# The first dense expert's two matrix products, split into two of 64 tokens each, for the lower and the upper output partitions in alternation

## The chip, the cores and the metric

The kernel is written in Bass, instruction by instruction for each engine, and runs on one core of a Trainium2 chip. The metric is the time of one execution on the device in microseconds (us), taken as the median of several runs. Rows of the profile come from one further execution that was recorded by the hardware profiler.

## The reference

A gated block on x of shape (4, 256, 256), that is 1024 tokens of 256 channels, in float32. First an additive adjacency step, then a mixture of experts with 32 experts of which each token uses 6, and a shared expert:

```python
x = x + tanh(g_xattn[0]) * L0_xattn_ref(ctx_512, layernorm(x), W, b)      # 0.6*sigmoid(si + sj + b) + 0.4*adj
x = x + tanh(g_ffn[0]) * L0_ffn_ref(layernorm(x), ...)
...
scores = sigmoid(xf @ w_router)                  # T = 1024 tokens, E = 32 experts
...                                              # best 4 of 8 groups, then best 6 experts in them
g = einsum('th,ehm->etm', xf, gate_w)            # H = 256, M = 176
u = einsum('th,ehm->etm', xf, up_w)
eo = einsum('etm,emh->eth', silu(g) * u, down_w)
routed = einsum('te,eth->th', combine, eo)
shared = silu(xf @ sh_gate_w) * (xf @ sh_up_w) @ sh_down_w
return routed + shared
```

## The kernel before

Tokens are handled 128 at a time (P = 128, J = 8 blocks). After the first residual step, the router and the shared expert, each token's row is scattered by GpSimd (`place`, L439) into a table in DRAM, `rows_dram`, once for each of its chosen experts, so that the rows of one expert lie together. Then the experts' work is done in **tiles** of 128 rows of one expert: ScalarE's queue fetches a tile (`load`, L282), TensorE transposes it (`transpose_x`, L759), multiplies it with the expert's gate and up weights (`gate_up`, L765), transposes the product (`turn_h`, L773) and multiplies it with the down weights (`down`, L779). ScalarE scales the result (L565), and GpSimd adds it into one of three sums in DRAM (`add`, L451). There are some 50 such tiles, ten to a round.

Two experts are left out of the tiles and treated **densely**, for all 1024 tokens, with a weight of zero where a token didn't choose them. The kernel finds the two that are used most. The first of them, which the change touches, is run **before** the tiles, straight from the transposed tokens `xnT`, by `gate_up_busy`, `turn_h_busy` and `down_busy`; the second after the tiles (L864, L873, L884).

For block j of 128 tokens of the first dense expert:

- `gate_up_busy(j)` makes 128 tokens by 352 columns (176 of gate, 176 of up) in the PSUM bank `pG[j % 2]`. The tokens (`xnT`) are the operand that TensorE loads as weights, 128 channels by 128 tokens; the expert's weights `busy_gu` are streamed past them. The 256 channels make two steps (k = 0, 1) that add up in PSUM.
- ScalarE takes the silu of the gate half (L569), VectorE multiplies (`gate_busy`, L1207).
- `turn_h_busy(j)` transposes the product in two steps of 88 columns (L796), and VectorE copies it into `hT` (L1211).
- `down_busy(j)` makes 128 tokens by 256 columns in `pY[j % 2]`, in two steps of 88 (L807). VectorE adds it to the tokens (`add_busy`, L1217).

TensorE's order in this stage is `gate_up_busy(0)`, and then for each j: `gate_up_busy(j + 1)`, `turn_h_busy(j)`, `down_busy(j - 1)`; the transposes of the first two tiles stand ahead of the last `down_busy`. Each engine works its own instructions in the order written and waits for others by semaphores.

In the trace's names several buffers share memory: `xg` in a row of L788 is `busy_gu`, `wd` in L807 is `busy_d`, `sup` is `hT`, `sdown` is `xT`, `sgate` is `sg` and `h`, `wgu` in rows ahead of the tiles is a buffer of the first step or of the shared expert. A row's operands carry their partitions and columns: 128*64 are weights of 64 columns. Each product of float32 appears in the trace as **two passes**, each with a load of weights (a row of PEld) and a MATMUL (a row of PE). So the two steps of one `gate_up_busy` are four passes, and so are those of one `down_busy`.

Some small products elsewhere serve as prices in what follows: products of the identity at the start (L629), transposes of ctx with 64 columns of weights (L635), the adjacency's scores (L645 with one streamed column, L648 with 256), and the table of tiles (L750 with 2 columns of weights, L752, L753). The program gives L635 the array's tile of 128 rows by 64 columns and L750 that of 128 by 32, both at column 0, and L629, L752 and L753 the whole array.

Two transfers hang on the end of this stage. SyncE's last group of expert weights waits for `s_by` to reach J, that is for the last `down_busy`, since their place is shared with `busy_d`. And ScalarE's queue issues the load of the fifth tile (`load(act, JH, JH)`) only behind the copies of the first two transposed tiles:

```python
            copy_xT(0, 0)
            copy_xT(1, 1)
            load(act, JH, JH)
            silu(0, 0)
```

Of the kernel before, what the change touches and what calls it, by code (L numbers as in the profile page):

```python
# [14 lines left out]
P = 128  # L15
# [16 lines left out]
def gated_xattn_moe(nc, x, ctx, g_xattn, g_ffn, w_adj, b_adj, w_router, corr_bias, gate_w, up_w, down_w,  # L32
                    sh_gate_w, sh_up_w, sh_down_w, out):
    B, N, H = x.shape
    D = ctx.shape[2]
    E, _, M = gate_w.shape
# [3 lines left out]
    K = H // P  # L40
    I = 2
    MI = M // I
# [28 lines left out]
    INTO_LAST = [0, 2, 1, 0, 2, 1, 0, 2, 1, 0]  # L71
    LEFT = sorted(range(SUMS), key=lambda i: max(s for s in range(ROUND) if INTO_LAST[s] == i))

    SECOND = [3, 5, 6, 7]
    PLACED = [range(0, GROUP), range(GROUP, JH), range(JH, J)]

    with ExitStack() as stack:
        def sb(name, shape, dt=F32):
            return stack.enter_context(nc.sbuf_tensor(name, shape, dt))

        def bank(name):
            return stack.enter_context(nc.psum_tensor(name, [P, 512], F32))
# [22 lines left out]
        xnT = sb("xnT", [P, K, T])  # L105
# [82 lines left out]
        hT = sup[:, :, :].rearrange("p k m -> p (k m)")[:, 0:4 * P].rearrange("p (a k t) -> p a k t", a=2, k=2)  # L188
# [5 lines left out]
        busy_gu = xg_own[:, :, :].rearrange("p i c -> p (i c)")[:, 0:2 * K * M].rearrange("p (g k m) -> p g k m", g=2, k=K)  # L194
        busy_d = wd[:, E - BATCH, :, :]
# [14 lines left out]
        pG = [bank(f"pG{i}") for i in range(2)]  # L210
        pH = [bank(f"pH{i}") for i in range(2)]
        pY = [bank(f"pY{i}") for i in range(2)]
# [171 lines left out]
        def _(pool):  # L384
# [37 lines left out]
            def second_rstd(b):  # L422
                g = slice(b * GROUP, (b + 1) * GROUP)
                pool.wait_ge(s_var, SECOND[b])
                pool.tensor_tensor(out=rstd2[:, g], in0=rstd2[:, g], in1=power[:, g], op=ALU.pow).then_inc(s_rstd, 1)
# [199 lines left out]
        def _(pe):  # L625
# [8 lines left out]
            for j in range(J):  # L634
                ins = nc.tensor.transpose(pX[j // 4][0:D, (j % 4) * P:(j % 4 + 1) * P], ctx_sb[:, j, :], ident[:, :])  # L635
# [6 lines left out]
            for c in range(2):  # L642
                pe.wait_ge(s_ctxTc, c + 1)
                for j in range(c * JH, (c + 1) * JH):
                    ins = nc.tensor.matmul(si_banks[c][:, j:j + 1], ctxT[:, j * P:(j + 1) * P], wij[:, 0:1], start=True, stop=True)  # L645
# [139 lines left out]

            def gate_up_busy(j):
                for k in range(K):
                    ins = nc.tensor.matmul(pG[j % 2][:, 0:2 * M].rearrange("t (g m) -> t g m", g=2),  # L788
                                           xnT[:, k, j * P:(j + 1) * P], busy_gu[:, :, k, :],
                                           start=(k == 0), stop=(k == K - 1))  # L790
                ins.then_inc(s_bgu, 1)

            def turn_h_busy(j):
# [6 lines left out]
            def down_busy(j):  # L800
                pe.wait_ge(s_bhTc, j + 1)
                if j < 2:
                    pe.wait_ge(s_shyc, J - 1 + j)
                else:
                    pe.wait_ge(s_byc, j - 1)
                for i in range(I):
                    ins = nc.tensor.matmul(pY[j % 2][:, 0:H], hT[0:MI, j % 2, i, :], busy_d[:, i, :],  # L807
                                           start=(i == 0), stop=(i == I - 1))
                ins.then_inc(s_by, 1)

            pe.wait_ge(s_busyw, 64)
            gate_up_busy(0)
            for j in range(J):
                if j + 1 < J:
                    gate_up_busy(j + 1)
                turn_h_busy(j)
                if j:
                    down_busy(j - 1)
            pe.wait_ge(s_tiles, 1)
            transpose_x(0, 1, 0)  # L820
            transpose_x(1, 1, 1)
            down_busy(J - 1)
            e_first = look_up(0)
            pe.wait_ge(s_ready, e_first + 1)
# [77 lines left out]
        def _(dve):  # L902
# [55 lines left out]
            def norm_group(b):  # L958
                dve.wait_ge(s_rstd, SECOND[b])
                for j in range(b * GROUP, (b + 1) * GROUP):  # L960
                    V.tensor_scalar(xn[:, j, :], xs[:, j, :], mv[:, j, 0:1], rstd2[:, j:j + 1],
                                    ALU.subtract, ALU.mult).then_inc(s_xn, 1)
# [345 lines left out]
```

## Time and profile before

| what | us |
|---|---|
| median of 3 runs | 249.18 (248.64 to 250.74) |
| the profiled execution's own time | 250.6 |
| its span, first to last instruction | 248.7 |
| TensorE busy in the span | 225.7 (91%) |
| first dense expert on TensorE, from its first pass to the first pass of the tiles | 67.48 to 86.24 |

The span is what the rows below divide. A busy time of TensorE counts from the start of a pass to its modelled end, and passes overlap, so the starts tell more than the durations.

### The profile page before, as it was taken

To read this page: it belongs to the slowest core of one execution; us is meant where nothing else is said; L and a number is where in the kernel's file an instruction comes from. 1 tells how busy PE (TensorE), PEld (TensorE's weight loads), DVE (VectorE), ACT (ScalarE), POOL (GpSimd) and SP (SyncE) were. 2 spreads that over 40 slices of the span, in tenths; PEclk is the share of its full clock that TensorE was granted. 3 is DMA by queue.
4 is the path that set the end of the run, shared out by engine and by line. 5 is a ranking of instruction groups with operands and counts; after the bars stand their busy time and mean duration, and the time that the engine had idled before them with its cause. 6 is when DMAs were issued, how large, how long until landed. Compare 5 with 4: busy or idle time off the path is not lost.

```text
span 248.7 us, 4830 instructions
## 1 busy us (share of the span) xinstructions
PE 225.7 (91%) x1051; PEld 175.0 (70%) x1052; DVE 130.5 (52%) x523; ACT 78.2 (31%) x220; POOL 137.1 (55%) x133
## 2 busy tenths in 40 slices
PE   7994998996899977988899999999999899999980
PEld 6893786884677754765677777777777678777760
DVE  2898588989744541333343434343434334442765
ACT  3635122110021121313435353444444344433220
POOL 6253747777777752344565657565656547565000
PEclk9778699999799996899999999999999999999996
DMA  6999999999999999799765658677666634447846
GB/s 203 279 284 304 407 372 346 319 359 329 337 374 344 367 227 327 164 269 227 141 110 116 112 103 154 111 130 105 114 108 121 104 36 59 55 55 116 259 138 225
DMA packets 39290, 51.67 MB, mean 208 GB/s; under 512 B 4942, under 2 KB 33710, under 8 KB 39270
## 3 DMA queue, kind: packets, MB, share of 16 engines
q1 hardware_dynamic: 24368, 29.81, 39.1%
q0 software_dynamic: 10416, 17.20, 34.1%
q10 hardware_dynamic: 4486, 4.44, 6.8%
q8 instruction: 7, 0.11, 0.2%
q14 instruction: 13, 0.11, 0.1%
HBM read 30.83 MB, written 20.61 MB: 207 GB/s over the span
## 4 chain that ended last, share of the span: by engine, by line
PE 67%; DVE 16%; DMA 5%; issue 4%; ACTq 3%; ACT 3%; POOL 1%; DVEq 1%
PE pG L765 21%; PE pY L779 15%; PE pG L704 5%; PE pX L759 4%; PE pH L773 4%; PE pG L864 4%; PE pG L788 4%; DMA xg<-rows_dram 3%; PE pY L715 3%; PE pY L807 2%; PE pY L884 2%; DVE xs L1267 2%; DMA wij<-in_L_xattn_W_dram 1%; ACTq L267 1%; ACTq L282 1%
## 5 line engine op out<-in xcount | busy, mean ns | idle before, releaser
L451 POOL DMA_INDIRECT sum_dram<-choice,idx x50 | 77.4, 1548 | 59.2 <-ACT choice L565 42.9
L765 PE MATMUL pG<-wgu,sdown 128*128 x200 | 69.8, 472 | 3.8 <-ACT sdown L553 2.8
L439 POOL DMA_INDIRECT rows_dram<-rows,row_i x48 | 47.0, 980 | 19.0 <-issue 14.1
L779 PE MATMUL pY<-wd,sup 88*128 x200 | 52.3, 384 | 0.0
L1193 DVE COPY sup<-pH 88x256 f32<-88x256 f32 x50 | 21.0, 420 | 55.1 <-PE pH L773 55.1
L765 PEld LDWEIGHTS pG<-wgu,sdown 128*128 128x128 f32 x200 | 35.1, 195 | 16.6 <-issue 6.2
L565 ACT ACTIVATE choice<-pY,wt 128x256 f32<-128x256 f32 x50 | 23.7, 473 | 55.3 <-PE pY L779 30.9
L779 PEld LDWEIGHTS pY<-wd,sup 88*128 88x128 f32 x200 | 34.6, 193 | 3.1
L773 PEld LDWEIGHTS pH<-ident,sgate 128*88 128x88 f32 x100 | 16.0, 161 | 12.5 <-issue 0.6
L558 ACT ACTIVATE sgate<-pG 128x176 f32<-128x176 f32 x50 | 15.9, 317 | 24.4 <-PE pG L765 23.6
L553 ACT ACTIVATE sdown<-pX 128x256 f32<-128x256 f32 x50 | 18.7, 376 | 7.9 <-PE pX L759 5.2
L773 PE MATMUL pH<-ident,sgate 128*88 128x128 f32 x100 | 19.4, 276 | 0.0
L1189 DVE TENSOR_TENSOR sgate<-sgate,pG 128x176 f32<-128x176 f32 x50 | 16.2, 325 | 5.9 <-ACT sgate L558 5.9
L704 PE MATMUL pG<-xnT,sgate 128*128 128x256 f32 (+1 forms) x48 | 14.6, 432 | 0.0
L715 PE MATMUL pY<-sdown,wgu 128*128 128x256 f32 (+1 forms) x48 | 12.8, 423 | 0.6 <-DVE wgu L1069 0.6
L704 PE MATMUL pG<-xnT,sup 128*128 128x256 f32 (+1 forms) x48 | 13.3, 403 | 0.0
L525 ACT ACTIVATE wgu<-pG 128x256 f32<-128x256 f32 (+1 forms) x12 | 4.6, 383 | 27.5 <-PE pG L704 27.5
L759 PEld LDWEIGHTS pX<-ident,rows 128*128 128x128 f32 x60 | 11.4, 196 | 2.0 <-issue 0.6
L715 PEld LDWEIGHTS pY<-sdown,wgu 128*128 128x128 f32 (+1 forms) x48 | 10.2, 214 | 2.5 <-DVE wgu L1069 0.8
L759 PE MATMUL pX<-ident,rows 128*128 128x128 f32 x60 | 11.6, 278 | 0.2 <-issue 0.2
L704 PEld LDWEIGHTS pG<-xnT,sup 128*128 128x128 f32 (+1 forms) x48 | 9.5, 198 | 2.1
L864 PE MATMUL pG<-wgu,xnT 128*128 x32 | 10.8, 460 | 0.0
(188 smaller groups left out, 275.9 us busy)
## 6 DMA issues: line engine op xcount, KB each, us to landing
wgu<-in_L_ffn_gate_w_dram SPq DMA_DIRECT2D x8, 704.0 KB, 10.8
wgu<-in_L_ffn_up_w_dram SPq DMA_DIRECT2D x8, 704.0 KB, 11.4
wd<-in_L_ffn_down_w_dram SPq DMA_DIRECT2D x8, 640.0 KB
sum_dram<-zeros POOLq DMA_DIRECT2D x3, 1152.0 KB, 13.1
rows<-rows_dram ACTq DMA_DIRECT2D x18, 144.5 KB, 3.6
rows_dram<-zeros SPq DMA_DIRECT2D x8, 289.0 KB, 3.9
rows<-sum_dram SPq DMA_DIRECT2D x8, 256.0 KB, 3.8
xg<-rows_dram ACTq DMA_DIRECT2D x12, 144.5 KB, 2.8
```

What stands on the lines that cost most here:

```text
L439: pool.indirect_dma_start(rows_dram[:, :], bass.IndirectOffsetOnAxis(ap=row_i[:, j, k:k + 1], axis=0), rows[:, j, :], None).then_inc(done, 16)
L451: pool.indirect_dma_start(sums_dram[into[s]][:, :], bass.IndirectOffsetOnAxis(ap=idx[:, s:s + 1], axis=0), y[s % YRING], None, compute_op= ...
L553: nc.scalar.activation(xT[:, par, :, :].rearrange("p k t -> p (k t)"), pX[par][:, 0:K * P], ACT.Copy).then_inc(s_xTc, 1)
L565: nc.scalar.activation(y[s % YRING], pY[s % 2][:, 0:H], ACT.Copy, scale=wt[:, s:s + 1]).then_inc(s_yc, 1)
L704: ins = nc.tensor.matmul(pG[u % 2][0:m, i * GROUP * P:(i + 1) * GROUP * P], w[:, k, c], xnT[:, k, b * GROUP * P:(b + 1) * GROUP * P], star ...
L715: ins = nc.tensor.matmul(pY[j % 2][:, 0:H], sh[0:m, b % 2, i, (j % GROUP) * P:(j % GROUP + 1) * P], sdown[0:m, i, :], start=(i == 0), stop ...
L759: ins = nc.tensor.transpose(pX[par][:, k * P:(k + 1) * P], xg[s][:, 0:H].rearrange("t (p k) -> t k p", k=K)[:, k, :], ident[:, :])
L765: ins = nc.tensor.matmul(pG[par][:, 0:2 * M].rearrange("t (g m) -> t g m", g=2), xT[:, par, k, :], wgu[:, bass.ds(e, 1), :, k, :].rearrang ...
L773: ins = nc.tensor.transpose(pH[par][0:MI, i * P:(i + 1) * P], h[:, par, :].rearrange("t (p i) -> t i p", i=I)[:, i, :], ident[:, :])
L779: ins = nc.tensor.matmul(pY[par][:, 0:H], hT[0:MI, par, i, :], wd[:, bass.ds(e, 1), i, :], start=(i == 0), stop=(i == I - 1))
L864: ins = nc.tensor.matmul(pG[j % 2][:, 0:2 * M].rearrange("t (g m) -> t g m", g=2), xnT[:, k, j * P:(j + 1) * P], wgu[:, bass.ds(e_common, ...
L1193: V.tensor_copy(hT[0:MI, par, :, :].rearrange("p i t -> p (i t)"), pH[par][0:MI, 0:I * P]).then_inc(s_hTc, 1)
```

## The change

Each product of `gate_up_busy` and of `down_busy` becomes two, one for tokens 0 to 63 of the block, which fills partitions 0 to 63 of the PSUM bank, and one for tokens 64 to 127, which fills partitions 64 to 127. For each step k (or i) the lower half is issued and then the upper half. Each half loads 64 columns of weights in place of 128, and streams the same 352 (or 256) columns past them. The program gives these halves the tile of 128 rows by 64 columns of TensorE's array, the lower at column 0 and the upper at column 64; all other products of the dense expert have the whole array of 128 by 128. Which instruction signals the other engines stays the same: the last of each group.

```diff
+    PARTED = [slice(0, P // 2), slice(P // 2, P)]
...
             def gate_up_busy(j):
                 for k in range(K):
-                    ins = nc.tensor.matmul(pG[j % 2][:, 0:2 * M].rearrange("t (g m) -> t g m", g=2),
-                                           xnT[:, k, j * P:(j + 1) * P], busy_gu[:, :, k, :],
-                                           start=(k == 0), stop=(k == K - 1))
+                    for part in PARTED:
+                        ins = nc.tensor.matmul(pG[j % 2][part, 0:2 * M].rearrange("t (g m) -> t g m", g=2),
+                                               xnT[:, k, j * P + part.start:j * P + part.stop], busy_gu[:, :, k, :],
+                                               start=(k == 0), stop=(k == K - 1))
                 ins.then_inc(s_bgu, 1)
...
                 for i in range(I):
-                    ins = nc.tensor.matmul(pY[j % 2][:, 0:H], hT[0:MI, j % 2, i, :], busy_d[:, i, :],
-                                           start=(i == 0), stop=(i == I - 1))
+                    for part in PARTED:
+                        ins = nc.tensor.matmul(pY[j % 2][part, 0:H], hT[0:MI, j % 2, i, part], busy_d[:, i, :],
+                                               start=(i == 0), stop=(i == I - 1))
                 ins.then_inc(s_by, 1)
```

On TensorE, from the shared expert's last product (`shared_down(3)`) into the third block of the dense expert, the order before is this (a row gives the line, output<-operands, output partitions x columns, and how many in a row):

```order
L715 MATMUL pY<-sdown,wgu 128x256 x6
L788 MATMUL pG<-xg,xnT 128x352 x4
L796 MATMUL pH<-ident,sgate 88x128 x2
L788 MATMUL pG<-xg,xnT 128x352 x2
L796 MATMUL pH<-ident,sgate 88x128 x2
L807 MATMUL pY<-wd,sup 128x256 x2
L788 MATMUL pG<-xg,xnT 128x352 x2
```

and after the change, at the same place (line numbers below the diff's first hunk are one higher, below the second two, and below the third three):

```order
L716 MATMUL pY<-sdown,wgu 128x256 x6
L790 MATMUL pG<-xg,xnT 64x352 x8
L798 MATMUL pH<-ident,sgate 88x128 x2
L790 MATMUL pG<-xg,xnT 64x352 x4
L798 MATMUL pH<-ident,sgate 88x128 x2
L810 MATMUL pY<-wd,sup 64x256 x4
L790 MATMUL pG<-xg,xnT 64x352 x4
```

Nothing changes its place. Every product of L788 and L807 stands twice, with 64 output partitions in place of 128. The other engines' instructions and their order are the same.

## Rows read from the trace of the kernel before

**Rows 1.** The page's first part: busy time, share of the span, instructions.

```profile
PE 225.7 (91%) x1051; PEld 175.0 (70%) x1052; DVE 130.5 (52%) x523; ACT 78.2 (31%) x220; POOL 137.1 (55%) x133
```

**Rows 2.** The chain that ended last: start us, us, what released the next.

```profile
86.50 8.10 DMA xg<-rows_dram
94.64 0.70 PE pX L759 x2
...
95.63 2.71 PE pG L765 x4
98.34 0.43 PE pH L773 x2
98.76 1.71 PE pY L779 x4
...
125.24 1.19 PE pG L765 x4
126.64 0.87 PE pY L779 x4
...
239.50 0.49 DVE xs L1256
```

**Rows 3.** TensorE's timeline from the dense expert on: start us, us, line, operation, idle before.

```profile
70.07 1.35 PE L788 MATMUL pG<-xg,xnT 128*128 128x352 f32 x4
71.25 0.38 PE L796 MATMUL pH<-ident,sgate 128*88 128x128 f32 x2
71.47 1.03 PE L807 MATMUL pY<-wd,sup 88*128 88x256 f32 x4
72.34 1.35 PE L788 MATMUL pG<-xg,xnT 128*128 128x352 f32 x4
...
91.04 1.03 PE L779 MATMUL pY<-wd,sup 88*128 x4
94.64 0.70 PE L759 MATMUL pX<-ident,xg 128*128 128x128 f32 x2 [2.57 <-DMA xg<-rows_dram]
```

**Rows 4.** TensorE's timeline at the start, same columns.

```profile
1.50 2.93 PE L629 MATMUL pH<-ident 128*128 128x128 f32 x12 [1.50 <-POOL ident L400]
4.22 1.81 PE L635 MATMUL pX<-ident,wgu 128*64 128x128 f32 x8
```

**Rows 5.** Line L635's passes: durations min/median/max ns, first and last start us.

```profile
L635 PE MATMUL pX<-ident,wgu x8: 313/421/421, 4.2 to 5.7; 128*64 128x128 f32 x8
```

**Rows 6.** Timeline again: products of one streamed column (PE), a group of weight loads (PEld).

```profile
6.27 1.05 PE L645 MATMUL pX<-wij,xnT 64*128 64x1 f32 x8
7.18 1.11 PE L648 MATMUL pG<-xnT,wj_wide 64*128 64x256 f32 x4
...
69.96 0.89 PEld L788 LDWEIGHTS pG<-xg,xnT 128*128 128x128 f32 x4
```

**Rows 7.** TensorE's timeline at the tile table, just before the dense expert.

```profile
61.75 0.27 PE L750 MATMUL pH<-ident,tile_of 128*2 128x128 f32 x1 [2.33 <-DVE tile_of L1171]
61.86 0.38 PE L752 MATMUL pH<-ident,limit 128*128 128x128 f32 x2
62.08 0.39 PE L753 MATMUL pH<-ident,low 128*128 128x128 f32 x2
```

**Rows 8.** ScalarE's tile loads (L282): four issued from 70 to 78, four from 86 to 93.

```profile
DMA to landing us min/median/max: 6.4/6.8/7.1
...
DMA to landing us min/median/max: 6.6/7.0/7.4
```

**Rows 9.** Stretches: busy time by engine, granted TensorE clock, DMA share, GB/s.

```profile
64.00:65.00 1.00, 1.00 (x4) 0.82 (x3) 0.93 (x4) 0.00 (x0) 0.69 (x2) 0.50 1.04 367
...
95.00:100.00 5.00, 4.72 (x12) 2.95 (x11) 1.00 (x4) 0.70 (x2) 1.61 (x1) 0.50 0.78 278
```

**Rows 10.** TensorE's timeline at the end of the tile loop's steady part.

```profile
197.64 0.50 PE L759 MATMUL pX<-ident,rows 128*128 128x128 f32 x2 [0.25 <-issue]
198.74 1.45 PE L765 MATMUL pG<-wgu,sdown 128*128 x4 [0.61 <-issue]
```

## The prediction

> **What bounds the kernel now.** I read the page's first part, then the chain that ended last, then TensorE's timeline of the stage that the change touches, and last the rows elsewhere that price a pass, a load of weights and a change of tile. TensorE is busy for 225.7 of 248.7 us [rows 1], and the chain shows that it is no mere average: inside the tile loop it goes from `gate_up` to `down` and back in turns of 2.5 us, and only the last sums, from 239.50 on, are VectorE's [rows 2]. In the dense stage TensorE never waits: four passes of `gate_up_busy` take 71.25 - 70.07 = 1.18 us, two transposes 0.22, four passes of `down_busy` 72.34 - 71.47 = 0.87, and the next turn starts without a gap [rows 3]. So whatever this stage gains or loses on TensorE moves its end at 86.24 by as much.
>
> Behind it stands the only slack. The fifth tile's load is issued at 86.50, behind the copies of the first two transposed tiles, and lands 8.10 us later [rows 2]. TensorE is out of work at 91.04 + 1.03 = 92.07, 5.57 after that issue, and waits 2.57 us [rows 3]. Then the granted clock is at its half level, 1.2 GHz (0.50) [rows 9]: the next `gate_up` takes 2.71 against 1.19, the transposes 0.43 against 0.22, the `down` 1.71 against 0.87 [rows 2, 3]. That is 1.52 + 0.21 + 0.84 = 2.6 us lost to the clock.
>
> **What a half costs by itself.** A pass streams as many columns as before; the question is whether 64 output tokens stream faster than 128. They don't: eight passes of L635, which load 64 columns, start 4.2 to 5.7, 0.21 us apart [rows 5], and twelve passes of L629 just before, of 128 columns and as many streamed, fill 1.50 to 4.22, 0.23 apart with the slow first one in it [rows 4]. So a half costs a whole pass, 0.295 in `gate_up_busy` and 0.217 in `down_busy`, and there are now 64 of each in place of 32. One after the other, that is 8 x 1.18 + 8 x 0.87 = 16.4 us more. All depends on whether the upper half streams while the lower one does.
>
> No row of this trace has a product at column 64 of the array, so I bound it. If the halves overlap, TensorE still takes its instructions in order: lower step 0, first pass and second pass, then upper, first and second. Both passes of a half use the same columns of the array, so the second waits for the first. What can overlap is the second pass of one half with the first of the next. A block of products with nothing before it then has starts at 0, p, p, 2p, 2p and so on (p is the length of a pass): as fast as before, but its last pass streams alone. The chip leaves this mode ten times (the products stand in ten runs between transposes; seven end in a `gate_up_busy`, three in a `down_busy`), which costs 7 x 0.295 + 3 x 0.217 = 2.7 us. That is the lower bound with overlap.
>
> To it comes the load of weights. A load starts when the pass before it has started and not earlier: the first load for a `gate_up_busy` begins at 69.96, 0.11 before its product at 70.07, when the second transpose pass begins [rows 3, 6]. Where a product streams only one column, loads set the pace: (7.18 - 6.27) / 8 = 0.114 for 128 columns [rows 6]. I take half of it, 0.057, for 64. In the changed stage the upper half's first pass waits that long after the lower half's second has begun, and so on at each of the 64 changes from half to half: 64 x 0.057 = 3.65, and the lone last passes count 0.057 less each: 7 x 0.238 + 3 x 0.160 = 2.15. The sum is **5.8 us**. With a load that costs as much as 128 columns it would be 8.9; with loads pulled ahead, 2.7.
>
> The Trainium skill, "TensorE: Matmul & The Clock Gate", Part 3, says that products in different column tiles run at once, start some 4 ns apart and measured 2.38 times faster for three of them; by its 4 ns the sum would be an estimated 2.9 us. No run here shows it yet.
>
> **What hides it.** The other engines have a turn of 2.27 us (70.07 to 72.34) for one block, and follow later, not sooner: no new wait. The load of the fifth tile and SyncE's last expert weights (which wait for the last `down_busy`) are issued later with the stage, and meet each other again. But the load stands ahead of the last `down_busy`, which grows by 0.39 (5 x 0.217 + 3 x 0.057 - 0.87), so TensorE now wants the tile 5.96 after the issue. Eight loads beside such weights landed in 6.4 to 7.4 us where the trace tells it [rows 8], this one in 8.1. I take 7.4, the slowest of the three others in the same burst. The wait is then 1.4 in place of 2.57: 1.1 back. With 8.1 it is 0.4 back, with 6.4 it is 2.1.
>
> Does the clock still fall? It was at 0.50 behind waits of 2.57 [rows 3, 9] and 2.33 [rows 7, 9], and passes keep their full pace behind waits of 0.25 and 0.61 [rows 10]. A wait of 1.4 lies between; I take it that it falls, as the long ones are the nearer in kind (a stage that has run dry), and give the other answer to a rival. The sum: 5.8 - 1.1 = **4.7 us later**.
>
> **The rivals.**
>
> (a) The halves overlap as above, but the clock holds: 4.7 - 2.6 = 2.1 later, 251.3. For it: most loads landed in 7 us or less, which makes the wait one of 1.0. Against it: the load in question was the slowest.
>
> (b) The halves don't overlap at all: the change doesn't do what its alternation is there for. 16.4 later on TensorE. GpSimd's scatters, which share the transfers, are over by then, so the wait may go altogether, and the slow clock with it: 16.4 - 2.57 - 2.6 = 11.2, up to 15.5 if only the longer last `down_busy` (0.87) is won back; 260.4 to 264.7, some 262. For it: nothing in this trace shows two products at once. Against it: passes already overlap with loads and with each other's ends [rows 3, 6].
>
> (c) A change of tile empties the array. The trace speaks against it: L635 has a tile of 64 columns and starts at 4.22, while the last whole-array pass before it ends at 4.43 [rows 4], and L752 starts at 61.86, 0.16 before the end of L750's tile of 32 columns, just as L753 starts 0.16 before L752's end [rows 7]. If it did, a pass's tail beyond its streaming (1.35 - 4 x 0.295 = 0.17 [rows 3]) would stand bare at 20 changes, 3.4 us: 8.1 later, 257.3. This rule is in the Trainium skill, "TensorEngine Tiling (Array Packing)", Key Properties: changing the tiling mode drains TensorE. By that rule the rows would show a gap that they don't, for a mode that stays at column 0.
>
> (d) Faster than before. The place is the fifth tile's load, the price the wait and the slow clock behind it, 2.57 + 2.6 = 5.2 us. If loads are pulled ahead (2.7 lost) and the tile lands within 6 us, the kernel ends 2.5 earlier, 246.7. It decides as soon as the stage loses less than 5.2 and the wait is gone; the loads' shortest time of 6.4 speaks against the second.
>
> **How the numbers follow.** The profiled execution took 250.6, its span and 1.9 around it; the median is 249.18, 1.4 below. The shifts are differences of the span, and I put them on the median: 249.2 + 4.7 = **253.9**. Chances: the forecast 0.34, (a) 0.26, (b) 0.25, (c) 0.08, (d) 0.07. A measurement of this kernel tells about 1% (2.5 us) from no change. Of (a) I count 0.06 as slower, since its loads may cost more (up to 8.9 in place of 5.8), the rest as the same; of (d) 0.04 as faster. So slower 0.34 + 0.25 + 0.08 + 0.06 = 0.73, the same 0.23, faster 0.04. The range reaches from 249.8, in the midst of what (a) may give with short loads, to 265, the end of (b); it leaves out (d) and the lower part of (a), and little above.
>
> **What would show it.** In the profile after, the passes at column 64 start 0.05 to 0.06 behind the lower half's second pass if the forecast is right, a whole pass behind if (b). The first pass of the transposes starts a whole pass, and no more, behind the last product (more: (c)). The dense stage, 18.76 us now, takes 24.5; 35 under (b), 21.5 under (d). The wait for the fifth tile is near 1.4, and the clock behind it 0.50; under (a) it stays at 1.00. The tile loop's turns of 2.5 us and the tail stay as they are. I am wrong if TensorE holds a half back for another reason (the order of the two passes of a product, the PSUM bank that both halves write), or if the granted clock falls within the stage.

## The result and the profile after

| what | before | after |
|---|---|---|
| median, us | 249.06 (20 runs, 246.2 to 252.61) | 252.39 (20 runs, 249.09 to 254.92) |
| the profiled execution's own time and its span, us | 250.6 and 248.7 | 250.42 and 248.6 |
| first dense expert on TensorE, first pass to first pass of the tiles | 67.48 to 86.24: 18.75 | 66.88 to 88.55: 21.67 |

The kernel became slower by 1.3%: the ratio is 1.0126, with a 95% interval of 1.0086 to 1.0167, that is 3.1 us (2.1 to 4.2). The medians are over all 20 runs, while the ratio leaves out those in a slower state of the chip (six of the kernel after), so it is a little below 252.39 / 249.06. The two profiled executions happen to be equally long, so the cause isn't read from their spans. It is read stage by stage, from the first pass of one stage to the first pass of the next, and checked against the medians.

The page's first part of the kernel after answers to [rows 1]. There are 64 more passes, 1115 in place of 1051, and TensorE is busy as long as before. Halves that streamed one behind the other would have added 16.4 us, so already here the second half of each product seems to cost no streaming of its own. (The two sums can't be compared to less than a few us, since the granted clock over the span was 0.944 before and 0.981 after.)

```profile
PE 225.8 (91%) x1115; PEld 170.0 (68%) x1116; DVE 130.3 (52%) x523; ACT 78.3 (31%) x220; POOL 137.3 (55%) x133
```

TensorE in the dense expert answers to [rows 3]. The first row is of the line's passes (durations min/median/max ns), the second of the timeline in a narrow stretch around the start of a `gate_up_busy`, the others of the timeline over a whole turn (start us, us, line, operation, count, idle before).

```profile
L790 PE MATMUL pG<-xg,xnT x64: 457/459/511, 66.9 to 83.7; 128*64 128x352 f32 x64
...
72.42 0.47 PE L790 MATMUL pG<-xg,xnT 128*64 128x352 f32 x2
...
72.42 1.35 PE L790 MATMUL pG<-xg,xnT 128*64 128x352 f32 x8
73.70 0.46 PE L798 MATMUL pH<-ident,sgate 128*88 128x128 f32 x2
74.09 1.08 PE L810 MATMUL pY<-wd,sup 88*64 88x256 f32 x8
75.01 1.35 PE L790 MATMUL pG<-xg,xnT 128*64 128x352 f32 x8
```

Eight passes of `gate_up_busy` take 1.35 us from start to end, exactly what four took before. The first two rows show why: a pass lasts 0.459, and two of them lie in 0.47. The lower and the upper half start 0.006 us apart (0.005 to 0.008 over all pairs of the stage) and stream together. But a turn lasts 75.01 - 72.42 = 2.59 in place of 2.27, and all of that sits at the seams, the places where split products meet transposes or whole products: 1.28 from the first product to the transposes (1.18 before), 0.39 over the two transposes (0.22), 0.92 over the down products (0.87). The loads of weights of the same turn show the first two of these:

```profile
73.02 0.14 PEld L790 LDWEIGHTS pG<-xg,xnT 128*64 128x64 f32 x2 [0.15 <-issue]
73.70 0.24 PEld L798 LDWEIGHTS pH<-ident,sgate 128*88 128x88 f32 x2 [0.55 <-issue]
74.09 0.20 PEld L810 LDWEIGHTS pY<-wd,sup 88*64 88x64 f32 x4
```

The pair of passes to which the loads of 73.02 belong starts at 73.31 and streams for 0.295, to 73.61. The transposes' load starts only at 73.70, at the same time as its product, 0.094 behind that end; within one shape such a load begins 0.11 ahead, when the pass before has just started [rows 3, 6]. Then the transposes' second pass follows 0.187 behind the first where 0.11 was usual, since its load too comes only now. Into the down products it is the same again. The number of loaded columns alone isn't the cause: before, products with 128 loaded columns and transposes with 88 follow each other without a gap [rows 3].

Behind the stage, TensorE at the tiles and the chain that ended last (start us, us, what released the next) answer to the ends of [rows 2, 3], and the granted clock of two stretches to [rows 9]:

```profile
88.55 1.45 PE L766 MATMUL pG<-wgu,sdown 128*128 x4
...
94.34 0.51 PE L760 MATMUL pX<-ident,xg 128*128 128x128 f32 x2
...
99.99 0.51 PE L760 MATMUL pX<-ident,xg 128*128 128x128 f32 x2 [2.17 <-DMA xg<-rows_dram]
100.94 1.45 PE L766 MATMUL pG<-wgu,sdown 128*128 x4 [0.45 <-ACT sdown L554]
```

```profile
92.38 7.57 DMA xg<-rows_dram
```

```profile
95.00:100.00 5.00, 2.54 (x11) 1.64 (x11) 1.51 (x7) 1.54 (x4) 1.61 (x1) 1.00 1.02 368
100.00:105.00 5.00, 4.55 (x21) 3.36 (x22) 1.00 (x4) 1.53 (x5) 1.59 (x1) 1.00 0.80 171
```

The fifth tile, issued at 88.78, is there when TensorE wants it at 94.34. The wait has moved to the sixth tile, whose load was issued at 92.38: 2.17 us, and the granted clock stays at 1.00 (2.4 GHz) in the stretch of the wait and behind it.

### The profile page after: what moved, and what is told of

It reads as the page before. It is cut to its first block, busy times and chain, and to the rows that moved or that the text cites. A ratio compares the mean times of both kernels' runs of the same rounds, so it can differ in the third digit from the quotient of the medians.

```text
span 248.6 us, 4958 instructions
## 1 busy us (share of the span) xinstructions
PE 225.8 (91%) x1115; PEld 170.0 (68%) x1116; DVE 130.3 (52%) x523; ACT 78.3 (31%) x220; POOL 137.3 (55%) x133
## 4 chain that ended last, share of the span: by engine, by line
PE 72%; DVE 13%; DMA 4%; ACTq 4%; issue 3%; ACT 2%; POOL 1%; DVEq 0%
PE pG L766 21%; PE pY L780 15%; PE pG L705 5%; PE pX L760 4%; PE pG L790 4%; PE pG L867 4%; PE pH L774 4%; PE pY L716 4%; PE pY L810 3%; DMA xg<-rows_dram 3%; PE pY L887 2%; DVE xs L1270 2%; ACTq L283 2%; ACTq L268 1%; PE pX L646 1%
## 5 line engine op out<-in xcount | busy, mean ns | idle before, releaser
L766 PE MATMUL pG<-wgu,sdown 128*128 x200 | 68.4, 465 | 4.2 <-ACT sdown L554 3.0
L780 PE MATMUL pY<-wd,sup 88*128 x200 | 51.5, 379 | 0.0
L766 PEld LDWEIGHTS pG<-wgu,sdown 128*128 128x128 f32 x200 | 34.3, 191 | 16.8 <-issue 6.2
L780 PEld LDWEIGHTS pY<-wd,sup 88*128 88x128 f32 x200 | 34.1, 190 | 2.9
L774 PE MATMUL pH<-ident,sgate 128*88 128x128 f32 x100 | 19.2, 273 | 0.0
L705 PE MATMUL pG<-xnT,sgate 128*128 128x256 f32 (+1 forms) x48 | 12.9, 391 | 0.4 <-DVE wgu L1072 0.4
L716 PE MATMUL pY<-sdown,wgu 128*128 128x256 f32 (+1 forms) x48 | 12.3, 409 | 0.3 <-DVE wgu L1072 0.3
L705 PE MATMUL pG<-xnT,sup 128*128 128x256 f32 (+1 forms) x48 | 12.3, 379 | 0.0
L1202 DVE COPY wt<-rows 128x1 f32 x30 | 4.6, 154 | 11.8 <-issue 11.8
```

Source lines behind the costliest of these rows:

```text
L705: ins = nc.tensor.matmul(pG[u % 2][0:m, i * GROUP * P:(i + 1) * GROUP * P], w[:, k, c], xnT[:, k, b * GROUP * P:(b + 1) * GROUP * P], star ...
L716: ins = nc.tensor.matmul(pY[j % 2][:, 0:H], sh[0:m, b % 2, i, (j % GROUP) * P:(j % GROUP + 1) * P], sdown[0:m, i, :], start=(i == 0), stop ...
L766: ins = nc.tensor.matmul(pG[par][:, 0:2 * M].rearrange("t (g m) -> t g m", g=2), xT[:, par, k, :], wgu[:, bass.ds(e, 1), :, k, :].rearrang ...
L774: ins = nc.tensor.transpose(pH[par][0:MI, i * P:(i + 1) * P], h[:, par, :].rearrange("t (p i) -> t i p", i=I)[:, i, :], ident[:, :])
L780: ins = nc.tensor.matmul(pY[par][:, 0:H], hT[0:MI, par, i, :], wd[:, bass.ds(e, 1), i, :], start=(i == 0), stop=(i == I - 1))
```

## The experiments

The questions were three: do the halves overlap and why, what are the 2.92 us if they do, and what becomes of the slack behind the stage. Times of single runs can't tell 3 us apart, so such runs are read by their stages. Two repeats come first, since they show how far one trace speaks for others.

**Two repeats.** `before_again` and `after_again` are the kernels before and after with a blank line added, for one more trace of each.

> The kernel before once more, for a second trace. If the wait for the fifth tile and the half clock behind it are usual, they stand there again, with 2 to 3 us of wait. If the clock's fall belonged to that one execution, the wait stands there and the clock stays at 1.00 behind it; then this execution is nearer the median of 249.1 than the 250.6 of the first profile.

> The changed kernel once more, for a second trace. The dense stage is 21.7 us again. If the wait of 2.2 us for the sixth tile in place of the fifth is the rule for the changed kernel, it stands there again; a clock at half level behind it would make this execution slower than the first one's 250.4 by some 2 us.

They took 251.61 and 254.91. The stages of all four traces, from first pass to first pass, in us (the second ten tiles, the rest and the tail agree within 0.15):

| | dense stage starts | dense stage | first ten tiles | second ten |
|---|---|---|---|---|
| before | 67.48 | 18.75 | 33.48 | 25.32 |
| before_again | 67.66 | 18.75 | 34.20 | 25.33 |
| after | 66.88 | 21.67 | 30.97 | 25.37 |
| after_again | 69.45 | 21.68 | 32.89 | 25.37 |

The dense stage is 2.92 longer, and each kernel repeats its own to 0.01 us. What differs between executions is the start of the stage, ahead of anything that the change touches (64.49 to 69.55 over all traces of this study), and the first ten tiles. TensorE's timeline and the granted clock at the late tile, first in `before_again`:

```profile
95.59 0.70 PE L760 MATMUL pX<-ident,xg 128*128 128x128 f32 x2 [3.08 <-DMA xg<-rows_dram]
96.53 2.71 PE L766 MATMUL pG<-wgu,sdown 128*128 x4 [0.24 <-issue]
...
95.00:100.00 5.00, 4.17 (x10) 2.53 (x11) 0.30 (x1) 0.70 (x2) 1.61 (x1) 0.50 0.94 337
```

and in `after_again`:

```profile
102.88 0.52 PE L761 MATMUL pX<-ident,xg 128*128 128x128 f32 x2 [3.00 <-DMA xg<-rows_dram]
...
100.00:105.00 5.00, 1.62 (x4) 1.15 (x5) 0.27 (x2) 0.77 (x2) 3.20 (x2) 0.82 0.83 249
105.00:108.00 3.00, 3.00 (x12) 2.02 (x11) 0.66 (x2) 0.32 (x1) 0.00 (x0) 0.72 0.98 240
```

Before, it is the fifth tile that is late, with the half clock behind it (a `gate_up` of 2.71). After, it is the sixth, by 2.17 in one trace and 3.00 in the other, and the second time the clock does fall. Of the 4.5 us between the two executions of the kernel after, 2.6 lie ahead of the dense stage and 1.9 in the first ten tiles, so neither tells what the change costs.

**Do the halves need the alternation?** `apart` issues all lower products and then all upper ones; `same_side` does the same, but the upper half too is written to partitions 0 to 63, over the lower's result, so that nothing is computed for tokens 64 to 127 of a block.

```diff
-                for k in range(K):
-                    for part in PARTED:
+                for part in PARTED:
+                    for k in range(K):
...
-                        ins = nc.tensor.matmul(pG[j % 2][part, 0:2 * M].rearrange("t (g m) -> t g m", g=2),
+                        ins = nc.tensor.matmul(pG[j % 2][PARTED[0], 0:2 * M].rearrange("t (g m) -> t g m", g=2),
```

(the first hunk in both functions and both kernels, the second, and its like in `down_busy`, in `same_side` alone)

> All products of the lower half first, then all of the upper half, so lower and upper no longer alternate. The dense stage (first pass of the dense expert to the first gate and up pass of the tiles) was 18.76 us before and 21.67 with alternation. If the two halves of the array take their passes each in their own order, independent of the program's order between them, the passes still start in pairs 6 ns apart and the stage stays at 21.7. If TensorE starts passes in the program's order, only neighbours overlap: of the eight passes of a block's gate and up products seven lengths are needed in place of four, and the stage is some 31 us (8 x 3 x 0.295 + 8 x 3 x 0.217 = 12.3 more than before, less what overlaps between products). The forecast's rule (program order, a load of weights between) belongs to the second.

> As the run with the halves apart, but both halves write partitions 0 to 63, so that both use columns 0 to 63 of the array; the upper half's result takes the place of the lower's, and the output is that of other numbers. No overlap is possible: all theories expect 18.76 + 16.4 = 35.2 us for the stage. They differ in the changes to and from the whole array: if any change between a tile of 64 columns and the whole array costs what the alternating kernel showed (0.32 us for entering and leaving, ten times), the stage is some 38; if only a tile at column 64 makes TensorE wait, as the rows of the kernel before with tiles at column 0 suggest, 35.2.

`apart` took 251.16 (before on the same chip: 248.75), its dense stage 21.99. TensorE's timeline of a turn, after a narrow stretch around its start:

```profile
74.10 0.52 PE L790 MATMUL pG<-xg,xnT 128*64 128x352 f32 x2
...
74.10 1.40 PE L790 MATMUL pG<-xg,xnT 128*64 128x352 f32 x8
75.43 0.46 PE L798 MATMUL pH<-ident,sgate 128*88 128x128 f32 x2
75.82 1.09 PE L810 MATMUL pY<-wd,sup 88*64 88x256 f32 x8
76.73 1.40 PE L790 MATMUL pG<-xg,xnT 128*64 128x352 f32 x8
```

Eight passes still lie in 1.40 us, and two in the first 0.52. The upper half's first pass starts 0.014 behind the lower's first although three passes of the lower half stand between them in the program; from the second pass on the distance is 0.055 (in `down_busy` it is 0.013 throughout). So the two column tiles take their passes independently of each other, and the alternation is worth 0.32 us of the whole stage. The Trainium skill says so in "TensorEngine Tiling (Array Packing)", Key Properties: different tiles can load weights and multiply in parallel. The Trainium skill, "TensorE: Matmul & The Clock Gate", Part 3, also says that products start strictly in program order; this trace disagrees, by the 0.014 where three passes of 0.295 would have stood. `same_side` took 266.49:

```profile
71.26 2.58 PE L790 MATMUL pG<-xg,xnT 128*64 128x352 f32 x8
73.77 0.46 PE L798 MATMUL pH<-ident,sgate 128*88 128x128 f32 x2
74.16 1.94 PE L810 MATMUL pY<-wd,sup 88*64 88x256 f32 x8
75.94 2.53 PE L790 MATMUL pG<-xg,xnT 128*64 128x352 f32 x8
```

Now eight passes take 2.58, one behind the other, and the stage 37.99. The overlap hangs on the second column of the array alone. And 37.99 is 18.75 + 16.4 (64 passes more, as the prediction worked out for rival (b)) + 2.84: the price at the seams stays when nothing is at column 64 and nothing overlaps. What differs from the whole products is then the tile of 64 columns alone.

**What is paid at the seams?** `gate_only` splits `gate_up_busy` alone, `down_only` the other alone. If the price goes with the number of split products, each has about half of it; if it goes with the number of times that TensorE changes from halves to whole products and back, each has all of it, as both kinds of products lie in the same stretch between transposes.

```diff
-                    for part in PARTED:
-                        ins = nc.tensor.matmul(pY[j % 2][part, 0:H], hT[0:MI, j % 2, i, part], busy_d[:, i, :],
-                                               start=(i == 0), stop=(i == I - 1))
+                    ins = nc.tensor.matmul(pY[j % 2][:, 0:H], hT[0:MI, j % 2, i, :], busy_d[:, i, :],
+                                           start=(i == 0), stop=(i == I - 1))
```

(`gate_only` against the kernel after; `down_only` puts back the other function)

> Only the gate and up products are split; the down products are whole again. If the price is one for each change of the tile (0.32 us for entering and leaving together), there are seven stretches of split products and the stage is 18.76 + 7 x 0.32 = 21.0 us. If the price goes with the number of split products (2.9 us over 16 products, 0.18 each), eight are left and it is 20.2. By the forecast's rule (loads of weights between halves, a lone last pass) 18.76 + 8 x 4 x 0.057 + 7 x 0.238 = 22.2.

> Only the down products are split. With a price for each change of the tile: eight stretches, 18.76 + 8 x 0.32 = 21.3 us. With a price for each split product: 20.2. By the forecast's rule 18.76 + 8 x 4 x 0.057 + 8 x 0.160 = 21.9.

They took 252.1 and 251.9, their stages 21.30 and 21.25. Eight stretches have a product of `down_busy` in them, and 18.75 + 8 x 0.32 is 21.3. Seven have one of `gate_up_busy`, which gives 21.0. `gate_only` is 0.3 above that since its first sixteen passes took 2.93 us where those of the kernel after took 2.52: the granted clock was 0.50 from 67.4 to 68.2. The turns tell it most plainly. `gate_only`:

```profile
75.88 1.40 PE L790 MATMUL pG<-xg,xnT 128*64 128x352 f32 x8
77.21 0.46 PE L798 MATMUL pH<-ident,sgate 128*88 128x128 f32 x2
77.51 1.03 PE L809 MATMUL pY<-wd,sup 88*128 88x256 f32 x4
78.47 1.40 PE L790 MATMUL pG<-xg,xnT 128*64 128x352 f32 x8
```

and `down_only`:

```profile
74.44 1.45 PE L789 MATMUL pG<-xg,xnT 128*128 128x352 f32 x4
75.73 0.38 PE L797 MATMUL pH<-ident,sgate 128*88 128x128 f32 x2
76.04 1.08 PE L809 MATMUL pY<-wd,sup 88*64 88x256 f32 x8
77.05 1.45 PE L789 MATMUL pG<-xg,xnT 128*128 128x352 f32 x4
```

A turn is 2.59 in the one and 2.61 in the other, as long as with both split (2.59), against 2.27 with none. With half of the split products all of the price is there: +0.32 for one way into the halves and one way out. In `down_only` the seam has moved to where `down_busy` meets `gate_up_busy`, whose first pass now stands longer (1.45 for four passes, 1.35 before). This seam also shows that TensorE isn't waiting for another engine there: `gate_up_busy` has no wait for a semaphore in it.

**Half as many seams.** `pairs_whole` and `pairs_split` work two blocks in one turn, with the kernel's products before and after, so that there are five stretches of products in place of ten.

```diff
+            for j in range(0, J, 2):
+                gate_up_busy(j)
+                gate_up_busy(j + 1)
                 if j:
+                    down_busy(j - 2)
                     down_busy(j - 1)
+                turn_h_busy(j)
+                turn_h_busy(j + 1)
```

(VectorE's order is changed alike)

> The kernel before with the dense expert's order changed to two blocks at a time (two gate and up products, two down products of the blocks before, then two blocks of transposes), on TensorE and in step on VectorE. It is the base for the next run; its stage is 18.8 us if nothing waits, a little more if the transposes wait for VectorE.

> The same order with the products split as in the change. The split products now stand in five stretches in place of ten. If the price is one for each change of the tile, the stage is 5 x 0.32 = 1.6 us longer than in the run without the split; if the price goes with the number of split products, 2.9 longer, as in the first order.

They took 248.6 and 254.56 in single runs. Most of these 6 us has nothing to do with the split: the stage starts at 64.49 in the one and at 69.55 in the other. The stages are 19.80 and 20.74. Two turns of `pairs_whole`, then of `pairs_split`:

```profile
72.69 2.53 PE L788 MATMUL pG<-xg,xnT 128*128 128x352 f32 x8
...
77.22 2.53 PE L788 MATMUL pG<-xg,xnT 128*128 128x352 f32 x8
```

```profile
78.23 2.59 PE L790 MATMUL pG<-xg,xnT 128*64 128x352 f32 x16
...
83.08 2.59 PE L790 MATMUL pG<-xg,xnT 128*64 128x352 f32 x16
```

A turn of two blocks is 4.53 and 4.85: +0.32 again, for twice the work. Over the whole stage the difference is 0.94 and not 5 x 0.32 = 1.6: the two turns in the middle bring 0.64, the first 0.16 and the end 0.14, because in this order TensorE stands idle at both ends (0.62 for VectorE at the first transposes of `pairs_whole`, 0.46 in `pairs_split`; some 0.3 ahead of the last down products of `pairs_whole`), which takes up a part.

**Why the rows of before showed no seam.** [Rows 4, 7] have a tile of 64 and one of 32 columns next to the whole array, and no gap. Both smaller ones are transposes. `ctx_matmul` is the kernel before with L635's transposes written as products with the identity.

```diff
-                ins = nc.tensor.transpose(pX[j // 4][0:D, (j % 4) * P:(j % 4 + 1) * P], ctx_sb[:, j, :], ident[:, :])
+                ins = nc.tensor.matmul(pX[j // 4][0:D, (j % 4) * P:(j % 4 + 1) * P], ctx_sb[:, j, :], ident[:, :],
+                                       start=True, stop=True)
```

> The kernel before, where the eight transposes of ctx at the start (64 columns of weights, a tile of 64 columns at column 0) are written as products with the identity, which give the same numbers. In the trace of before the transposes follow the whole-array products ahead of them without a gap (first start at 4.22, 0.21 after the last one's). If a transpose takes no tile of its own and so needs no change, while a product with 64 columns of weights does, a gap of some 0.1 us at the half pace of that stretch or more appears ahead of the first of these products, and its second pass starts late by a load of weights. If the changes are free at column 0 for whatever reason, the first product starts as the transposes did. The whole time moves by less than 0.5 us either way.

It took 248.84 (before in the same batch 250.35, 247.48 to 252.15; no difference was to be seen there). The loads of the kernel before, and then products and loads of `ctx_matmul` (L629 stands there as in [rows 4]):

```profile
4.11 1.57 PEld L635 LDWEIGHTS pX<-ident,wgu 128*64 128x64 f32 x8
```

```profile
4.36 2.48 PE L635 MATMUL pX<-ident,wgu 128*64 128x128 f32 x16
...
4.36 2.24 PEld L635 LDWEIGHTS pX<-ident,wgu 128*64 128x64 f32 x16 [0.22 <-issue]
```

As a transpose, L635 loads its first weights at 4.11, while L629's last pass is running, and starts at 4.22 [rows 4]. As a product it loads at 4.36, at the moment it starts, and it starts 0.14 later; its second pass follows 0.268 behind the first where 0.213 was usual. That is the seam, at column 0, without any second half. The transfer of ctx isn't what it waits for: it had landed at 3.9. The count tells one thing more: eight transposes were eight passes, eight products are sixteen.

Behind its first microseconds `ctx_matmul` is the kernel before, so it is a third trace of that kernel's tiles:

```profile
93.93 0.60 PE L760 MATMUL pX<-ident,xg 128*128 128x128 f32 x2 [1.75 <-DMA xg<-rows_dram]
94.87 2.71 PE L766 MATMUL pG<-wgu,sdown 128*128 x4 [0.34 <-issue]
```

Its dense stage is 18.75 as in the other two, but the fifth tile's wait is 1.75 here, with the slow clock behind it all the same, and the first ten tiles take 30.71, less than in either trace of the kernel after.

**What hides it?** Behind the stage TensorE waits for a tile. `early_one` issues the fifth tile's load ahead of the two copies; `early_whole` does so for the fifth and the sixth; `early_split` is `early_whole` with the split products.

```diff
+            load(act, JH, JH)
+            load(act, JH + 1, JH + 1)
             copy_xT(0, 0)
             copy_xT(1, 1)
-            load(act, JH, JH)
             silu(0, 0)
...
-                    turn(i, s, left=2 * ROUND, old=i, fetch=[n for n in FETCH if FETCH[n] == i * ROUND + s])
+                    turn(i, s, left=2 * ROUND, old=i, fetch=[n for n in FETCH if n > JH + 1 and FETCH[n] == i * ROUND + s])
```

(`early_one` has only the first of the added lines, and no second hunk)

> The kernel before, with the loads of the fifth and sixth tile issued by ScalarE right behind its last silu of the dense expert, ahead of the copies of the first two tiles (their buffers are free once the last gate and up product is done). If the wait for the fifth tile (2.57 us in the profile of before) and the slow clock behind it (2.6 us) are on the path, the kernel gets faster by 2 to 5 us. If the loads land no earlier, since the expert weights or the scatters hold them up, nothing changes.

> The change with the same early loads. If the change's 2.9 us in the dense stage were partly hidden by the wait for the fifth and sixth tile, nothing hides them now, and this is 2.9 us slower than the run with early loads and whole products, though faster than the change itself. If the change's loss comes from elsewhere (more waits for transfers, the clock), the two differ by some other amount.

> The kernel before with only the fifth tile's load issued early, behind the last silu of the dense expert. If the fifth tile's wait is all that the early loads removed, this is as fast as the run with two early loads (246.4) or a little faster, since ScalarE's copies of the first two tiles are held up by one load and not by two. If the sixth tile's load, which is then again issued late, takes the wait over as it did in the changed kernel, it is between 246.4 and 249.

| | median, us | against the kernel before | dense stage | first ten tiles |
|---|---|---|---|---|
| early_whole | 246.38 (6 runs) | 0.9868 (0.9818 to 0.9918) | 18.90 | 28.16 |
| early_split | 248.84 (12 runs) | 1.0019 (0.9985 to 1.0052) | 21.68 | 27.35 |
| early_one | 249.87 (12 runs) | 1.0026 (0.9986 to 1.0066) | 18.75 | 31.97 |

Each ratio is to runs of the kernel before on the same chip. The two chips differ (medians of before 248.92 beside `early_whole` and `early_split`, 250.35 beside `early_one`), so the first column isn't compared between them.

`early_whole` is faster than the kernel before by 1.3% (0.8 to 1.8), some 3.3 us by the ratio and 2.5 in the medians. Its fifth and sixth tile start without a wait, and the clock holds:

```profile
93.69 0.39 PE L760 MATMUL pX<-ident,xg 128*128 128x128 f32 x2
...
96.19 0.39 PE L760 MATMUL pX<-ident,xg 128*128 128x128 f32 x2
...
95.00:100.00 5.00, 4.56 (x22) 3.31 (x21) 2.00 (x8) 2.16 (x7) 0.61 (x1) 1.00 1.03 373
```

A part of what it gains in the first ten tiles is lost again in the second ten, which take 26.42 against 25.32 before (26.14 in `early_split`). In `early_one` the sixth tile, whose load is issued at 89.61, takes the fifth's place, and the slow clock with it, and no gain is left that these runs could tell:

```profile
97.43 0.61 PE L759 MATMUL pX<-ident,xg 128*128 128x128 f32 x2 [2.64 <-DMA xg<-rows_dram]
98.38 2.71 PE L765 MATMUL pG<-wgu,sdown 128*128 x4 [0.34 <-issue]
```

And where almost nothing waits behind the stage, the split costs 248.84 - 246.38 = 2.5 us in the medians (3.8 by the two ratios, whose intervals leave some 1.5 either way), with the dense stage 2.78 longer.

## Why the prediction was right, and where its steps were not

The forecast was +4.7 and 253.9; the medians say +3.3 and 252.39, the ratio +3.1. Sign, size and range held, but that the size did is in part luck. Of the sum's two terms, the 5.8 of the stage was twice the 2.92 measured, by a mechanism that isn't there, and of the 1.1 that the wait was to give back the medians show nothing (the interval leaves room for 0.8). The two errors go in opposite directions.

- **TensorE bounds the stage and never waits in it.** Right, but for 0.13 us at the last transposes of before, which wait for VectorE (a row of the weight loads of before, start us, us, idle before). All 2.92 us that the stage grew by are TensorE's.

```profile
83.74 0.25 PEld L796 LDWEIGHTS pH<-ident,sgate 128*88 128x88 f32 x2 [0.29 <-DVE sgate L1207]
```

- **A half costs a whole pass.** Right, and shown by `same_side`: 64 passes more, one after the other, cost 16.4 of its 19.2.
- **"TensorE still takes its instructions in order".** This step failed, and with it the whole of the 5.8: no lone last pass (2.15 in the sum), and no load at the changes from half to half (3.65). The order written doesn't hold between the two column tiles: the halves run 0.006 apart, and 0.013 to 0.057 apart when the program's order is against it. The price of a load was sized well (0.057 for 64 columns; 0.052 measured), but it is paid at the ten entries and not at 64 changes. The 2.9 that the prediction gave by the 4 ns of the Trainium skill, "TensorE: Matmul & The Clock Gate", Part 3, agrees with the 2.92 measured by accident: it too consisted of lone last passes, which aren't there. The distance of some 4 ns itself is near the 6 measured.
- **Rival (c), a change of tile empties the array.** This was the true mechanism, with a chance of 0.08. It was excluded by [rows 4, 7], and these are transposes, which `ctx_matmul` shows to be the exception. The change costs 0.094 from the end of the streaming to the first load, and then that load can't be hidden: the second pass comes 0.052 late with 64 columns of weights, 0.080 with the transposes' 88, 0.105 with 128. Into the halves and out to the transposes that is 0.146 + 0.174 = 0.32, ten times 3.2; of this the 0.094 ahead of the first product and the 0.105 behind the first pass of the tiles lie outside the two starts between which the stage is measured, so some 3.0 is left. The 2.92 found is a little less, as the seam at the last transposes takes up the 0.13 for which TensorE waited there before. The rival priced its 20 changes at 3.4, near the truth though by another quantity (a pass's tail of 0.17 at each), and put them on top of the 5.8 that isn't there. That changing the tiling mode drains TensorE stands in the Trainium skill, "TensorEngine Tiling (Array Packing)", Key Properties, and for products these runs agree, with the 0.094 by which the first load lies behind the streaming. A transpose with a tile of 64 columns at column 0 doesn't do it in the trace of before. A row that had the seam was in that trace and was not looked at: L648 is a product with a tile of 64 rows. The whole array's load behind its second group starts 0.13 after its streaming ends (two of its passes, 0.427 apart, and the loads that follow):

```profile
9.69 1.05 PE L648 MATMUL pY<-xnT,wj_wide 64*128 64x256 f32 x2
...
10.68 0.50 PEld L629 LDWEIGHTS pH<-ident 128*128 128x128 f32 x2 [0.65 <-issue]
```

- **What hides it.** Forecast: the fifth tile's wait shrinks from 2.57 to 1.4, with the half clock behind it. Instead it went from the fifth tile (0 left) to the sixth (2.17 and 3.00), and the clock stayed at 1.00 in one trace and fell in the other. The first ten tiles took 33.48, 34.20 and 30.71 in three traces of the order before (the third is `ctx_matmul`), and 30.97, 32.89 and 32.47 in three of the split one (the third is `apart`): 0.7 shorter on average, far less than the 3.5 by which traces of one kernel differ. The medians differ by as much as the stage has grown. How much is hidden on average stays open. `early_one` shows the mechanism by which it needn't be much: a tile made earlier uncovers the next.
- **The clock.** The forecast took a fall behind a wait of 1.4 as likely. It fell behind waits of 2.33 [rows 7, 9], 2.57 [rows 3, 9], 2.64, 3.00 and 3.08, and also behind 1.75 (`ctx_matmul`) and 1.32 (`pairs_whole`, 0.50 from 108 to 110); it held behind 2.17 (the trace after) and 2.19 (`same_side`, 1.00 from 60 to 67). So the length of the wait alone doesn't tell, and the price of 2.6 us for the clock is paid in some executions and not in others.
- **Rivals (a), (b) and (d).** (b) is refuted by the pairs of passes that start 0.006 apart, and by `same_side`, which shows what it would have cost. (a) and (d) had the wrong price on TensorE; the clock of (a) came true in one of two traces. (d)'s place is real, too: `early_whole` takes 2.5 us (3.3 by its ratio) there without the split.

Also open in part is why the dense stage starts anywhere from 64.49 to 69.55 us. The three earliest starts, up to 66.0, are those of `pairs_whole`, `apart` and `same_side`, in whose traces alone the granted clock held at 1.00 from 60 to 67; in the others it was 0.60 to 0.91 there. What sets the rest isn't shown. It adds to the spread of the medians' runs, and nothing in this change touches what lies ahead of it.

## What to carry to other kernels

A product that already fills the 128 columns of the array gains nothing from being split over two column tiles: the halves do run at once, but each streams as much as the whole did. What is left is the price at each seam with a product or transpose in another tile shape, here 0.15 to 0.20 us each and 0.32 to 0.34 for both ways, whatever the number of products between; so what is split should stand together. And when a wait for a transfer stands behind a stage, look at the next transfers in the queue as well: moving one load earlier gave nothing that could be measured, moving two gave 1.3%.

## What was not expected of the hardware

- Two column tiles of the array take their passes independently: with three passes of the other half in between by program order, the upper half started 0.014 us behind the lower.
- Between a product of one tile shape and a product or transpose of another no weights are loaded ahead: the first load began 0.094 us after the end of the streaming before it (0.14 at L635), where within one shape loads lie a whole pass ahead.
- A float32 transpose with a tile of 64 columns behind whole-array products has no such gap (load at 4.11, 0.11 ahead of its start), and is one pass where the same work written as a product is two.
